# A graph network's attention stage: four message rows multiplied in one VectorE instruction

## The chip, the cores and the metric

The kernel runs on one core of a Trainium2 chip. The metric is the device time of one execution in microseconds. Five engines work side by side, each through its own list in order: TensorE (PE), VectorE (DVE), ScalarE (ACT), GpSimd (POOL) and SyncE (SP). They meet only at semaphores.

## The reference

Four graph layers run one after the other over 6,250 nodes with 256 features and 100,000 edges sorted by destination. Each layer's result is added to its input and normalized. The change touches the first layer only, an attention layer of eight heads:

```python
h = jnp.einsum('nf,fhd->nhd', x, W)
a_src = jnp.sum(h * att_src, axis=-1)
a_dst = jnp.sum(h * att_dst, axis=-1)
e = jax.nn.leaky_relu(a_src[src] + a_dst[dst], NEG_SLOPE)
e_max = jax.ops.segment_max(e, dst, num_segments=N)
e_exp = jnp.exp(e - e_max[dst])
denom = jax.ops.segment_sum(e_exp, dst, num_segments=N)
alpha = e_exp / (denom[dst] + 1e-16)
msg = h[src] * alpha[:, :, None]
out = jax.ops.segment_sum(msg, dst, num_segments=N)
```

Each edge fetches the row of its source node, scales each of the eight heads' 32 features by a weight of that edge, and is summed into its destination.

## The kernel before

The edges are cut into steps of 128, such that all edges of a step end in one tile of 128 nodes. There are 832 steps (`STEPS_PAD`), in 52 groups of 16 (`GROUP`, `S`). The first layer's edge stage, called the heads stage here, does for each step `i`:

- GpSimd gathers the 128 source rows (264 floats each) from a table in memory, one indirect DMA per step (line 1024), into a ring `rows0` of 48 steps. Gather `t` waits for the product of step `t - 48`.
- VectorE multiplies the row's 256 features by the edge's eight weights, each spread over 32 features (line 1339). Both operands are in SBUF.
- TensorE multiplies a one-hot matrix of the destinations by the weighted rows (line 1297). The product goes to one of four banks (`BANKS0`), so it waits for the add of step `i - 4`.
- VectorE adds the product to the sums of the step's node tile (line 1322), three steps later (`LAG0`). The address of the tile is in a register. Each add waits for the product and for the add before it.

The weights of a group's 16 steps come from a chain of small operations (`chain_vector`, `chain_scalar`, `chain_tensor`) that all engines run one group ahead, spread over the 16 steps `k` of the group before: VectorE opens it at `k = 0` (line 1203) once the group's 16 gathers have landed, scans at 3, works on one row at 6 (line 1218, behind ScalarE's line 1119, behind TensorE's transposes at `k = 4`), scans again at 11, and ends it at 13 and 14. The weights of group `g + 1` are made by line 1107 before its first multiply. At the first step of each group the sums are rescaled (lines 1314 and 1316). When a node tile has got its last step, it is closed over the next eight steps, one or two small VectorE operations per step (`close_vector`), and there are 49 such closings.

VectorE's order in a step is: multiply, chain piece, add, closing piece. It is written out by hand, and so is every engine's. Tile numbers reach VectorE by a load of 16 registers (`load_ranks`), once in a group at `k = 11`; one register of them also chooses the column block of `adst` that line 1241 adds.

The other layers use passes of their own (from about 1,236 us on), whose adds share `load_ranks` with the heads stage. A second stage of interest for its rows is the last pass, where line 2015 is a VectorE operation with two SBUF inputs, and line 1863 the gather.

Of the kernel before, what the change touches and what calls it, by code (L numbers as in the profile page):

```python
# [9 lines left out]
ALU = mybir.AluOpType  # L10
# [3 lines left out]
P = 128  # L14
NODES = 6250
EDGES = 100000
FEAT = 256
# [7 lines left out]
GROUP = 16  # L25
# [98 lines left out]
def bcast(ap, axis, shape):  # L124
    return ap.unsqueeze(axis).to_broadcast(shape)
# [134 lines left out]
def build(nc, io):  # L260
    ctx = ExitStack()
    with ctx:
# [569 lines left out]
        def load_ranks(e, name, t0):  # L832
            if name not in rank_regs:
                rank_regs[name] = [e.alloc_register(f"rank{k}") for k in range(2 * GROUP)]
            a = t0 % (2 * GROUP)
            e.load(rank_regs[name][a:a + GROUP], rank_row[0:1, t0:t0 + GROUP])
# [33 lines left out]
        def rank_value(e, name, t):  # L870
            return e.snap(rank_regs[name][t % (2 * GROUP)], min_val=0, max_val=NODE_TILES - 1)
# [8 lines left out]
        BANKS0, LAG0 = 4, 3  # L880
# [100 lines left out]
        def close_scalar(e, i):  # L981
# [15 lines left out]
            "capped first over_in back_states states level_in level_out second_up second node bent_node larger below_node "  # L997
# [7 lines left out]
        weighted0 = s_weighted.take(STEPS_PAD)  # L1005
# [192 lines left out]
        def chain_vector(e, g, k):  # L1198
# [33 lines left out]
            if k == 11:  # L1232
                e.wait_ge(*ch_a.at("begin_col", g))
                e.tensor_tensor_scan(second[:, 0:P], turned3[:, 0:P], turned3[:, 2 * P:3 * P], begin_col[:, 0:1],
# [4 lines left out]
                load_ranks(e, "vector", g * S)  # L1239
                v = rank_value(e, "vector", g * S)  # L1240
                e.tensor_tensor(node_both.rearrange("p (k h) -> p k h", k=2),
                                bank_c[:, 264:264 + 2 * H].rearrange("p (k h) -> p k h", k=2),
                                bcast(adst[:, bass.DynSlice(v * H, H)], 1, [P, 2, H]),
                                ALU.add).then_inc(*ch_v.done("node"))
# [40 lines left out]
        def heads_tensor(e):  # L1285
# [4 lines left out]
            for i in range(STEPS_PAD):  # L1290
# [3 lines left out]
                e.wait_ge(*weighted0(i))  # L1294
# [7 lines left out]
        def heads_vector(e):  # L1302
# [5 lines left out]
            def add(i):  # L1308
                g = i // S
                if i % S == 0 and g:  # L1310
                    e.wait_ge(*ch_v.at("shrink", g))
# [22 lines left out]
            for i in range(STEPS_PAD):  # L1334
                g, k = i // S, i % S
                row = rows0[:, i % (3 * S), :]
                v = row[:, 0:FEAT].rearrange("p (h d) -> p h d", h=H)
                e.wait_ge(*ch_a.at("weights", g))
                e.tensor_tensor(v, v, bcast(row[:, FEAT:ROW0], 2, [P, H, D]), ALU.mult).then_inc(*weighted0.up)  # L1339
# [904 lines left out]
```

## Time and profile before

| | us |
|---|---|
| median of 3 executions | 5310.18 |
| lowest, highest | 5306.78, 5315.72 |
| the profiled execution | 5315.72 |
| its span in the trace | 5313.9 |
| first multiply and last add of the heads stage | 151.5, 1228.6 |
| first gather of the next pass | 1236.1 |

| engine, 900 to 1050 us | busy us of 150 |
|---|---|
| TensorE | 125.92 |
| VectorE | 125.53 |
| ScalarE | 99.94 |
| GpSimd | 114.95 |

An engine's busy time leaves out loads of registers and the issue of instructions. So GpSimd shows 77% busy where gathers follow one another without a pause other than their issue. Instructions of VectorE overlap at their ends: what one adds to the time is the distance from its start to the next one's start, not its duration. "Issue" stands for idle time that nothing in the profile explains.

### The profile page before, as it was taken

What the parts mean: (1) busy time and instruction counts of PE and PEld (TensorE: products, weight loads), DVE (VectorE), ACT (ScalarE), POOL (GpSimd) and SP (SyncE); (2) the same over time, 40 slices, a digit from 0 to 9 for tenths busy, and PEclk for the clock granted to TensorE, in tenths of its full rate; (3) what the DMA queues carried; (4) which work ended last, traced back from release to release, by engine and by line L of the source; (5) the groups of instructions that cost most, each with busy time, mean ns of one, the idle gap of its engine ahead of it and who ended that gap; (6) DMA issues with size and microseconds to landing.
All of it is one profiled execution on the core that took longest, in us unless ns stands there. A gap on an engine that the chain in (4) does not pass through costs nothing.

```text
span 5313.9 us, 86764 instructions
## 1 busy us (share of the span) xinstructions
PE 3931.6 (74%) x13357; PEld 2389.2 (45%) x13357; DVE 3517.2 (66%) x10780; ACT 2554.6 (48%) x6938; POOL 3875.0 (73%) x3995
## 2 busy tenths in 40 slices
PE   6888888887777777677777777777677656666763
PEld 4666666664444444344444443343333333444442
DVE  6789888885554545444444445666666578888887
ACT  1667667664555555455545552000000166666665
POOL 3777777775777777677777776777777677777775
PEclk8889889988899998887777777877888777777776
DMA  5444444443333333443333333333333322222222
GB/s 151 113 122 126 122 126 124 120 121 98 111 112 112 111 112 111 118 139 111 111 112 112 111 112 100 109 109 109 109 108 109 98 57 57 57 57 57 57 57 68
DMA packets 252628, 549.14 MB, mean 103 GB/s; under 512 B 71467, under 2 KB 136235, under 8 KB 252108
## 3 DMA queue, kind: packets, MB, share of 16 engines
q0 software_dynamic: 178752, 478.34, 32.8%
q1 hardware_dynamic: 66972, 58.64, 3.5%
q10 hardware_dynamic: 6384, 6.62, 0.5%
q8 instruction: 157, 2.57, 0.2%
q14 instruction: 363, 2.97, 0.2%
HBM read 501.16 MB, written 42.15 MB: 102 GB/s over the span
## 4 chain that ended last, share of the span: by engine, by line
PE 32%; POOL 22%; DMA 18%; issue 13%; DVE 6%; ACT 6%; SPq 2%; DVEq 1%; ACTq 0%; POOLq 0%
PE bank L1453 18%; POOL scratch L1863 12%; DMA scratch<-tab_x,src_idx 10%; POOL scratch L1399 9%; DMA scratch<-tab_h,src_idx 7%; PE bank L1297 4%; PE bank L172 4%; PE bank L1154 3%; DVE reg_acc L1463 2%; ACT scratch L1066 2%; POOL reg_x L1024 2%; SPq L865 1%; DVE reg_acc L1322 1%; PE bank L1142 1%; PE bank L157 1%
## 5 line engine op out<-in xcount | busy, mean ns | idle before, releaser
L1453 PE MATMUL bank<-scratch 128*128 x4986 | 1946.5, 501 | 739.9 <-SPq L1414 356.6
L1463 DVE TENSOR_TENSOR reg_acc<-reg_acc,bank 128x256 f32 x2493 | 1047.3, 420 | 1368.2 <-PE bank L1453 1310.3
L1399 POOL DMA_INDIRECT scratch<-tab_x,src_idx x1566 | 1494.3, 954 | 533.5 <-issue 259.4
L1453 PEld LDWEIGHTS bank<-scratch 128*128 128x128 f32 x4986 | 961.2, 229 | 1630.2 <-issue 1582.6
L1024 POOL DMA_INDIRECT reg_x<-tab_h,src_idx x832 | 838.7, 1008 | 302.7 <-issue 184.1
L1399 POOL DMA_INDIRECT scratch<-tab_h,src_idx x783 | 746.6, 953 | 264.7 <-issue 153.0
L1863 POOL DMA_INDIRECT scratch<-tab_h,src_idx x783 | 743.0, 949 | 249.3 <-issue 226.8
L1916 PE MATMUL bank<-reg_w,scratch 128*128 128x260 f32 x1664 | 639.8, 527 | 282.7 <-issue 180.1
L1423 ACT ACTIVATE scratch<-iota_row,dst_loc 128x128 f32<-128x128 f32 x1662 | 579.6, 393 | 345.5 <-PE bank L1453 336.1
L1297 PE MATMUL bank<-reg_x,scratch 128*128 128x265 f32 x1664 | 582.4, 461 | 72.7 <-DVE reg_x L1339 70.4
L1916 PEld LDWEIGHTS bank<-reg_w,scratch 128*128 128x128 f32 x1664 | 376.3, 252 | 505.1 <-issue 305.0
L1946 ACT ACTIVATE edge_w<-scratch,attr 128x68 f32 x832 | 288.3, 346 | 311.8 <-SPq L1877 282.0
L1297 PEld LDWEIGHTS bank<-reg_x,scratch 128*128 128x128 f32 x1664 | 305.0, 216 | 205.3 <-DVE reg_x L1339 174.5
L1322 DVE TENSOR_TENSOR reg_acc<-reg_acc,bank 128x265 f32 x832 | 353.5, 425 | 34.2 <-PE bank L1297 23.1
L2032 DVE TENSOR_TENSOR reg_acc<-reg_acc,bank 128x260 f32 x832 | 349.2, 420 | 15.7 <-issue 4.2
L1339 DVE TENSOR_TENSOR reg_x<-reg_x 128x256 f32<-128x256 f32 x832 | 342.6, 412 | 0.4 <-ACT reg_x L1107 0.4
L1439 DVE TENSOR_SCALAR scratch<-iota_row,dst_loc,edge_w 128x128 f32<-128x128 f32 x831 | 322.3, 389 | 6.1 <-issue 6.1
L1931 ACT ACTIVATE scratch<-iota_row,dst_loc 128x128 f32<-128x128 f32 x832 | 319.7, 386 | 3.1 <-DMA tab_h<-reg_w 1.6
L1767 ACT ACTIVATE adst<-adst,small 128x1 f32<-128x1 f32 x49 | 14.4, 294 | 617.4 <-DVE adst L1807 617.4
L2015 DVE SCALAR_TENSOR_TENSOR reg_w<-scratch,attr,edge_w 128x68 f32<-128x68 f32 x832 | 236.3, 284 | 99.9 <-ACT edge_w L1946 87.3
L2063 DVE TENSOR_TENSOR reg_w<-reg_w,bank 128x520 f32<-128x520 f32 x416 | 285.6, 686 | 0.4
L1428 ACT ACTIVATE scratch<-scratch 128x512 f32<-128x512 f32 x416 | 261.7, 629 | 13.1
(313 smaller groups left out, 4364.1 us busy)
## 6 DMA issues: line engine op xcount, KB each, us to landing
scratch<-tab_x,src_idx POOLq DMA_INDIRECT x1566, 2.8
scratch<-tab_h,src_idx POOLq DMA_INDIRECT x1566, 2.7
reg_x<-tab_h,src_idx POOLq DMA_INDIRECT x832
tab_h<-scratch ACTq DMA_DIRECT2D x7, 924.0 KB, 5.2
reg_x<-in_x SPq DMA_DIRECT2D x7, 896.0 KB, 11.3
reg_w<-in_x SPq DMA_DIRECT2D x49, 128.0 KB, 2.3
tab_x<-reg_acc SPq DMA_DIRECT2D x49, 128.0 KB
tab_xs<-reg_w SPq DMA_DIRECT2D x49, 128.0 KB, 2.6
```

Of the source, the lines that this page charges most:

```text
L1024: e.indirect_dma_start(rows0[:, t % (3 * S), 0:ROW0], None, tab_h0, bass.IndirectOffsetOnAxis(ap=src_idx[:, t:t + 1], axis=0)).then_inc(*g ...
L1297: e.matmul(psum[i % BANKS0][:, 0:W0_ROW], hots0[:, i % (2 * S), :], rows0[:, i % (3 * S), :], start=True, stop=True).then_inc(*product0.up)
L1322: e.tensor_tensor(v, v, psum[i % BANKS0][:, 0:W0_ROW], ALU.add).then_inc(*added0.up)
L1339: e.tensor_tensor(v, v, bcast(row[:, FEAT:ROW0], 2, [P, H, D]), ALU.mult).then_inc(*weighted0.up)
L1399: e.indirect_dma_start(ring_rows[:, j % SLOTS, :], None, self.table, bass.IndirectOffsetOnAxis(ap=src_idx[:, j:j + 1], axis=0)).then_inc(* ...
L1423: e.activation(ring_hots[:, i % HOTS, :], iota_row[:, :], ACT.Abs, scale=-1.0, bias=dst_loc[:, i:i + 1]).then_inc(*self.far.up)
L1439: e.tensor_scalar(ring_hots[:, i % HOTS, :], iota_row[:, :], dst_loc[:, i:i + 1], edge_w[:, i:i + 1], ALU.is_equal, ALU.mult).then_inc(*se ...
L1453: e.matmul(self.bank(i), ring_hots[:, i % HOTS, :], rows, start=True, stop=True).then_inc(*self.product.up)
L1463: e.tensor_tensor(v, v, self.bank(i), ALU.add).then_inc(*self.added.up)
L1863: e.indirect_dma_start(ring_rows[:, j % SLOTS, 0:ROW3], None, tab_h3, bass.IndirectOffsetOnAxis(ap=src_idx[:, j:j + 1], axis=0)).then_inc( ...
L1916: e.matmul(psum[i % BANKS][:, 0:WIDE3], hots3[:, i % HOTS, :], scaled3[:, i % 4, :], start=True, stop=True).then_inc(*product3.up)
L2032: e.tensor_tensor(v, v, psum[i % BANKS][:, 0:WIDE3], ALU.add).then_inc(*added3.up)
```

## The change

The weighting of four steps becomes one instruction over four rows of the ring (`AT_ONCE0`), issued at steps 0, 4, 8 and 12 of a group, and TensorE waits for the group of four. The node operation of the chain at `k = 11` moves ahead of the two scans and gets its tile number by a load of one register. The load of 16 registers moves to the add of a group's first step, and holds 16 registers instead of 32.

```diff
--- before.py
+++ after.py
@@ -831,9 +831,9 @@
 
         def load_ranks(e, name, t0):
             if name not in rank_regs:
-                rank_regs[name] = [e.alloc_register(f"rank{k}") for k in range(2 * GROUP)]
-            a = t0 % (2 * GROUP)
-            e.load(rank_regs[name][a:a + GROUP], rank_row[0:1, t0:t0 + GROUP])
+                rank_regs[name] = [e.alloc_register(f"rank{k}") for k in range(GROUP)]
+            n = min(GROUP, STEPS_PAD - t0)
+            e.load(rank_regs[name][0:n], rank_row[0:1, t0:t0 + n])
 
         slot_regs = {}
 
@@ -868,7 +868,7 @@
             return e.snap(end_regs[c % ENDS_AT_ONCE], min_val=1, max_val=STEPS)
 
         def rank_value(e, name, t):
-            return e.snap(rank_regs[name][t % (2 * GROUP)], min_val=0, max_val=NODE_TILES - 1)
+            return e.snap(rank_regs[name][t % GROUP], min_val=0, max_val=NODE_TILES - 1)
 
         def sums_of(e, i, a, b):
             return reg_acc[:, bass.DynSlice(rank_value(e, "vector", i) * ACC_W + a, b - a)]
@@ -877,7 +877,7 @@
 
         S, H, D = GROUP, HEADS0, HEAD0_DIM
         W0_ROW = FEAT + H + 1
-        BANKS0, LAG0 = 4, 3
+        BANKS0, LAG0, AT_ONCE0 = 4, 3, 4
         rows0 = reg_x[:, 0:3 * S * W0_ROW].rearrange("p (s f) -> p s f", f=W0_ROW)
         hots0 = reg_a[:, 0:2 * S * P].rearrange("p (s f) -> p s f", f=P)
         hots_t = reg_a[:, 2 * S * P:2 * S * P + 1024].rearrange("p (s f) -> p s f", s=2)
@@ -994,7 +994,7 @@
 
         got0 = [s_group[k].take(S * len(range(k, GROUPS, 3))) for k in range(3)]
         ch_v = s_chain["vector"].named(
-            "capped first over_in back_states states level_in level_out second_up second node bent_node larger below_node "
+            "capped first over_in back_states states level_in level_out node second_up second bent_node larger below_node "
             "part_added larger_added shrink_less bent shrink below", GROUPS)
         ch_t = s_chain["tensor"].named(
             "turned3 hots0 hots1 dst0 tails hots2 dst1 hots3 begins dst2 dst3 larger", GROUPS)
@@ -1002,7 +1002,7 @@
             "upright hot0 kept3 hot1 kept_hot0 step_masks hot2 kept_tails kept_hot1 hot3 begins kept_hot2 kept_hot3 "
             "begin_col part shrink weights", GROUPS)
         far0 = s_far.take(STEPS_PAD)
-        weighted0 = s_weighted.take(STEPS_PAD)
+        weighted0 = s_weighted.take(STEPS_PAD // AT_ONCE0)
         product0, added0 = s_edge.take(STEPS_PAD), s_added.take(STEPS_PAD)
         scaled0, denscaled0 = s_scaled.take(GROUPS - 1), s_denscaled.take(GROUPS - 1)
 
@@ -1230,18 +1230,20 @@
                                 ALU.max).then_inc(*ch_v.done("level_in"))
                 e.tensor_copy(level[:, (g + 1) % 2, 0:H], st[:, 0, S - 1, :]).then_inc(*ch_v.done("level_out"))
             if k == 11:
+                if "head" not in rank_regs:
+                    rank_regs["head"] = e.alloc_register("head_rank")
+                e.load(rank_regs["head"], rank_row[0:1, g * S:g * S + 1])
+                v = e.snap(rank_regs["head"], min_val=0, max_val=NODE_TILES - 1)
                 e.wait_ge(*ch_a.at("begin_col", g))
+                e.tensor_tensor(node_both.rearrange("p (k h) -> p k h", k=2),
+                                bank_c[:, 264:264 + 2 * H].rearrange("p (k h) -> p k h", k=2),
+                                bcast(adst[:, bass.DynSlice(v * H, H)], 1, [P, 2, H]),
+                                ALU.add).then_inc(*ch_v.done("node"))
                 e.tensor_tensor_scan(second[:, 0:P], turned3[:, 0:P], turned3[:, 2 * P:3 * P], begin_col[:, 0:1],
                                      ALU.add, ALU.max).then_inc(*ch_v.done("second_up"))
                 e.tensor_tensor_scan(second[:, P:2 * P][:, back], turned3[:, P:2 * P][:, back],
                                      turned3[:, 2 * P:3 * P][:, back], begin_col[:, 1:2], ALU.add,
                                      ALU.max).then_inc(*ch_v.done("second"))
-                load_ranks(e, "vector", g * S)
-                v = rank_value(e, "vector", g * S)
-                e.tensor_tensor(node_both.rearrange("p (k h) -> p k h", k=2),
-                                bank_c[:, 264:264 + 2 * H].rearrange("p (k h) -> p k h", k=2),
-                                bcast(adst[:, bass.DynSlice(v * H, H)], 1, [P, 2, H]),
-                                ALU.add).then_inc(*ch_v.done("node"))
                 e.wait_ge(*ch_v.at("node", g))
                 leaky(e, node_both).then_inc(*ch_v.done("bent_node"))
                 e.wait_ge(*ch_v.at("second", g))
@@ -1291,7 +1293,7 @@
                 g, k = i // S, i % S
                 if g + 1 < GROUPS:
                     chain_tensor(e, g + 1, k, True)
-                e.wait_ge(*weighted0(i))
+                e.wait_ge(*weighted0(i // AT_ONCE0))
                 if i >= BANKS0:
                     e.wait_ge(*added0(i - BANKS0))
                 e.matmul(psum[i % BANKS0][:, 0:W0_ROW], hots0[:, i % (2 * S), :], rows0[:, i % (3 * S), :], start=True,
@@ -1307,7 +1309,10 @@
 
             def add(i):
                 g = i // S
+                if i % S == 0 and g == 0:
+                    load_ranks(e, "vector", 0)
                 if i % S == 0 and g:
+                    load_ranks(e, "vector", i)
                     e.wait_ge(*ch_v.at("shrink", g))
                     e.wait_ge(*added0(i - 1))
                     v = sums_of(e, i, 0, FEAT).rearrange("p (h d) -> p h d", h=H)
@@ -1333,10 +1338,12 @@
                 chain_vector(e, 0, k)
             for i in range(STEPS_PAD):
                 g, k = i // S, i % S
-                row = rows0[:, i % (3 * S), :]
-                v = row[:, 0:FEAT].rearrange("p (h d) -> p h d", h=H)
-                e.wait_ge(*ch_a.at("weights", g))
-                e.tensor_tensor(v, v, bcast(row[:, FEAT:ROW0], 2, [P, H, D]), ALU.mult).then_inc(*weighted0.up)
+                if k % AT_ONCE0 == 0:
+                    rows = rows0[:, i % (3 * S):i % (3 * S) + AT_ONCE0, :]
+                    v = rows[:, :, 0:FEAT].rearrange("p s (h d) -> p s h d", h=H)
+                    e.wait_ge(*ch_a.at("weights", g))
+                    e.tensor_tensor(v, v, bcast(rows[:, :, FEAT:ROW0], 3, [P, AT_ONCE0, H, D]),
+                                    ALU.mult).then_inc(*weighted0.up)
                 if g + 1 < GROUPS:
                     chain_vector(e, g + 1, k)
                 if i >= LAG0:
```

VectorE's order, as the program has it, from step 14 of a group (line 1269 in the old numbering, 1271 in the new) into step 1 of the next. Line 1322 is the add (1327 in the changed kernel), 1339 the multiply (1345), 1203 the chain's opening; `ISA` computes an address from a register. Before:

```order
L1322 TENSOR_TENSOR reg_acc<-reg_acc,bank 128x265
L1339 TENSOR_TENSOR reg_x<-reg_x 128x256
L1269 TENSOR_TENSOR scratch<-scratch 128x128
L871 ISA
L1322 TENSOR_TENSOR reg_acc<-reg_acc,bank 128x265
L1339 TENSOR_TENSOR reg_x<-reg_x 128x256
L871 ISA
L1322 TENSOR_TENSOR reg_acc<-reg_acc,bank 128x265
L1339 TENSOR_TENSOR reg_x<-reg_x 128x256
L1203 TENSOR_TENSOR scratch<-reg_x,scratch 128x128
L871 ISA
L1322 TENSOR_TENSOR reg_acc<-reg_acc,bank 128x265
```

And changed:

```order
L1327 TENSOR_TENSOR reg_acc<-reg_acc,bank 128x265
L1271 TENSOR_TENSOR scratch<-scratch 128x128
L871 ISA
L1327 TENSOR_TENSOR reg_acc<-reg_acc,bank 128x265
L871 ISA
L1327 TENSOR_TENSOR reg_acc<-reg_acc,bank 128x265
L1345 TENSOR_TENSOR reg_x<-reg_x 128x4x256
L1203 TENSOR_TENSOR scratch<-reg_x,scratch 128x128
L871 ISA
L1327 TENSOR_TENSOR reg_acc<-reg_acc,bank 128x265
```

One multiply of 4x256 stands where four stood, one per step, and the adds of steps 1 to 3 behind it have no multiply between them.

VectorE at `k = 11`, from the second pair of scans (lines 1234 and 1236; 1242 and 1244 in the changed kernel) to the operation before the next add; `TENSOR_LOAD` is the load of tile numbers, and 1241 (1238) the node operation. Before:

```order
L1234 SCALAR_TENSOR_TENSOR scratch<-scratch 128x128
L1236 SCALAR_TENSOR_TENSOR scratch<-scratch 128x128
L836 TENSOR_LOAD step_rows
L871 ISA
L1241 TENSOR_TENSOR scratch<-bank,adst 128x16
L1196 SCALAR_TENSOR_TENSOR scratch<-scratch 128x16
L1248 TENSOR_TENSOR scratch<-scratch 128x128
L1251 TENSOR_TENSOR scratch<-scratch 128x8
```

And changed:

```order
L1235 TENSOR_LOAD step_rows
L1238 ISA
L1238 TENSOR_TENSOR scratch<-bank,adst 128x16
L1242 SCALAR_TENSOR_TENSOR scratch<-scratch 128x128
L1244 SCALAR_TENSOR_TENSOR scratch<-scratch 128x128
L1196 SCALAR_TENSOR_TENSOR scratch<-scratch 128x16
L1250 TENSOR_TENSOR scratch<-scratch 128x128
L1253 TENSOR_TENSOR scratch<-scratch 128x8
```

The load and the node operation now stand ahead of the scans, and the load takes one register.

VectorE at `k = 3`, from the first pair of scans to the first add of a group, with the rescaling (lines 1314 and 1316; 1319 and 1321) between. Before:

```order
L1207 SCALAR_TENSOR_TENSOR scratch<-scratch 128x128
L1208 SCALAR_TENSOR_TENSOR scratch<-scratch 128x128
L871 ISA
L1314 TENSOR_TENSOR reg_acc<-reg_acc,scratch 128x256
L871 ISA
L1316 TENSOR_TENSOR reg_acc<-reg_acc,scratch 128x8
L871 ISA
L1322 TENSOR_TENSOR reg_acc<-reg_acc,bank 128x265
L942 RECIPROCAL small<-small 128x8
```

And changed:

```order
L1207 SCALAR_TENSOR_TENSOR scratch<-scratch 128x128
L1208 SCALAR_TENSOR_TENSOR scratch<-scratch 128x128
L836 TENSOR_LOAD step_rows
L871 ISA
L1319 TENSOR_TENSOR reg_acc<-reg_acc,scratch 128x256
L871 ISA
L1321 TENSOR_TENSOR reg_acc<-reg_acc,scratch 128x8
L871 ISA
L1327 TENSOR_TENSOR reg_acc<-reg_acc,bank 128x265
```

The load of 16 registers now stands between the scans and the rescaling.

## Rows read from the trace of the kernel before

**Rows 1.** Gathers of the heads stage, groups of instructions from 150 to 1230 us.

```profile
L1024 POOL DMA_INDIRECT reg_x<-tab_h,src_idx x802 | 795.7, 992 | 244.4 <-issue 175.2 <-PE bank L1297 69.2
```

**Rows 2.** GpSimd's waits in the whole program: total us, times, longest us.

```profile
POOL reg_x L1024 <- issue: 184.1, 604, 0.3
POOL reg_x L1024 <- PE bank L1297: 69.2, 227, 0.3
```

**Rows 3.** VectorE's waits from 150 to 1230 us: total us, times, longest us.

```profile
DVE scratch L1218 <- ACT scratch L1119: 50.1, 37, 2.9
DVE scratch L1203 <- DMA reg_x<-tab_h,src_idx: 38.8, 21, 3.3
DVE reg_acc L1322 <- PE bank L1297: 23.1, 35, 1.8
DVE scratch L1241 <- issue: 6.2, 14, 1.0
```

**Rows 4.** Instructions of line 1203, 150 to 1230 us: ns min/median/max, first to last start.

```profile
L1203 DVE TENSOR_TENSOR scratch<-reg_x,scratch x51: 277/283/293, 153.9 to 1195.5; 128x128 f32<-128x128 f32 x51
```

**Rows 5.** Timeline of GpSimd (two gathers) and VectorE (line 1203): start, duration.

```profile
1003.07 1.07 POOL L1024 DMA_INDIRECT reg_x<-tab_h,src_idx  x1 [0.30 <-issue]
...
1006.00 0.29 DVE L1203 TENSOR_TENSOR scratch<-reg_x,scratch 128x128 f32<-128x128 f32 x1 [2.01 <-DMA reg_x<-tab_h,src_idx]
...
1188.38 1.20 POOL L1024 DMA_INDIRECT reg_x<-tab_h,src_idx  x1 [0.30 <-issue]
```

**Rows 6.** Timeline of VectorE in mid-stage, one multiply between the two.

```profile
1010.40 0.42 DVE L1322 TENSOR_TENSOR reg_acc<-reg_acc,bank 128x265 f32 x1
...
1011.08 0.42 DVE L1322 TENSOR_TENSOR reg_acc<-reg_acc,bank 128x265 f32 x1
```

**Rows 7.** Timeline of VectorE at the end of the program.

```profile
5272.42 2.01 DVE L2108 TENSOR_TENSOR reg_acc<-reg_acc,edge_w 128x1792 f32<-128x1792 f32 x1
5274.36 2.04 DVE L230 BATCH_NORM_STATS2 scratch<-reg_x 128x6 f32<-128x256 f32 x6
```

**Rows 8.** Timeline of VectorE, the last two adds of the heads stage.

```profile
1227.94 0.43 DVE L1322 TENSOR_TENSOR reg_acc<-reg_acc,bank 128x265 f32 x1 [0.22 <-DVE reg_acc L1322]
1228.59 0.43 DVE L1322 TENSOR_TENSOR reg_acc<-reg_acc,bank 128x265 f32 x1 [0.22 <-DVE reg_acc L1322]
```

**Rows 9.** Timeline of VectorE, one operation of a tile closing among the steps.

```profile
1196.78 0.42 DVE L946 TENSOR_TENSOR reg_acc<-reg_acc,small 128x256 f32<-128x256 f32 x1
1197.11 0.42 DVE L1339 TENSOR_TENSOR reg_x<-reg_x 128x256 f32<-128x256 f32 x1
```

**Rows 10.** Timeline of VectorE: a 16-register load (first pair), a one-register load (second).

```profile
4448.28 0.28 DVE L2015 SCALAR_TENSOR_TENSOR reg_w<-scratch,attr,edge_w 128x68 f32<-128x68 f32 x1
4449.17 0.43 DVE L2027 TENSOR_TENSOR reg_acc<-reg_acc,adst 128x260 f32 x1 [0.60 <-issue]
...
93.06 0.21 DVE L812 COPY edge_w<-bank 128x64 f32<-128x64 f32 x1
93.41 0.36 DVE L801 COPY adst<-scratch 128x392 f32 x1
```

**Rows 11.** Timeline of VectorE: the first of two scans, and what follows both.

```profile
1008.44 0.41 DVE L1207 TENSOR_TENSOR_SCAN scratch<-scratch 128x128 f32<-128x128 f32 x1
...
1009.09 0.40 DVE L1314 TENSOR_TENSOR reg_acc<-reg_acc,scratch 128x256 f32 x1
```

**Rows 12.** Instructions of the last pass, 4400 to 5200 us.

```profile
L1863 POOL DMA_INDIRECT scratch<-tab_h,src_idx x639 | 606.5, 949 | 194.8 <-issue 184.1 <-SPq L1875 10.7
L2015 DVE SCALAR_TENSOR_TENSOR reg_w<-scratch,attr,edge_w 128x68 f32<-128x68 f32 x680 | 193.1, 284 | 66.3 <-ACT edge_w L1946 54.6 <-issue 9.6
```

**Rows 13.** Timeline of GpSimd and VectorE as the heads stage begins.

```profile
112.47 14.12 POOL L1024 DMA_INDIRECT reg_x<-tab_h,src_idx  x1 [0.30 <-issue]
114.20 11.15 DVE L1325 MEMSET reg_acc<- 128x13312 f32 x1 [2.70 <-issue]
```

**Rows 14.** TensorE's wait for the multiplies, 150 to 1230 us.

```profile
PE bank L1297 <- DVE reg_x L1339: 70.4, 147, 2.2
```

## The prediction

> **What bounds the kernel now.** Only the heads stage is changed, some 1,080 of 5,314 us; what follows starts when its sums are complete. What the stage's own engines do decides it, so I ask first who sets the pace there. In the groups of instructions GpSimd's gathers come first: 802 of them take 795.7 us and the idle time before them 244.4 us, together 1,040.1 us, or 1.297 us a gather and 20.75 us for a group of 16 [rows 1]. Then I look at what GpSimd waited for. No gap is longer than 0.3 us, whether it is put down to issue (184.1 us over 604 times, 0.305 each) or to a product (69.2 over 227, 0.305 each): the named product lands inside a gap that is there anyway [rows 2]. The ring of 48 steps never holds a gather up. GpSimd runs without a stop and nothing in this change shortens its list.
>
> VectorE follows. From the first to the last opening of a chain are 50 groups in 1195.5 - 153.9 = 1,041.6 us, 20.83 us a group [rows 4], the same pace. In the list of its waits 38.8 us (21 times) are for gathers, 0.76 us a group over 51 [rows 3]. Without them it would need 20.83 - 0.76 = 20.07 us. Its other waits are for the chain: 50.1 us for line 1119's tails, 23.1 us for products [rows 3]. So the bound is GpSimd by a small margin: VectorE may grow by 20.75 - 20.07 = 0.68 us a group before the stage gets longer, and if it shrinks, it waits more for gathers.
>
> **Part 1, the batch.** Two adds with one multiply between are 11.08 - 10.40 = 0.68 us apart, so each instruction of 256 elements costs 0.34 us on VectorE, though it lasts 0.42 [rows 6]. A product over 1,792 elements with the same kind of spread operand lasts 2.01 us, and its follower starts 1.94 us after it [rows 7]. Between the two sizes that is (1.94 - 0.34) / 1,536 = 1.042 ns an element, so 1,024 elements cost 0.34 + 768 x 0.001042 = 1.14 us. Four multiplies cost 1.36 us. The batch saves 0.22 us, 0.88 us a group, 46 us over 208 batches if VectorE were the bound. The bounds of this price are an exact 0.34 for the fixed part (saving 46) and the full duration of each (4 x 0.42 [rows 9] against 0.42 + 0.80 = 1.22: 0.46 a batch, 96 us); I take the first, since the starts show the overlap.
>
> The Trainium skill, "VectorE: DVE Perf Modes", section on the TRN2 errata, says that many small tiles pay the SBUF latency each and a large one once, and gives (N + 151) / 0.96 ns for such an fp32 operation. For the durations the trace agrees: 2.02 us for 1,792 elements against the row's 2.01. By it the batch would save 3 x 157 = 472 ns. The distance of the starts says that half of that is already hidden.
>
> **Part 2, adds that stand behind one another.** This is what the diff does not say. Each add waits for the add before it. Today a multiply stands between, which hides the wait. Where nothing did, the adds were 1228.59 - 1227.94 = 0.65 us apart, 0.22 of it idle and put down to the add itself [rows 8], against 0.34. Each bare pair costs 0.31 us. A batch leaves three pairs bare, 12 a group: the adds of steps 1-3, 5-7, 9-11, 13-15. Chain work longer than 0.31 stands before those of 3, 6, 11 and 13, and before that of 14 stands a small operation of about 0.20. Seven are bare: 7 x 0.31 + 0.11 = 2.28 us. Closings fill some: each runs over eight steps, four of them with an operation of 0.33 us [rows 9], four with about 0.1, so a closing hides up to 4 x 0.31 + 4 x 0.1 = 1.64 us, and 7 of 16 steps need it: 0.72 x 49 / 52 = 0.68 us. Left: 1.60 us a group.
>
> **Part 3, the loads.** With 16 registers loaded between, two starts are 0.89 us apart, of which 0.60 idle; with one register 0.35, of which 0.14 idle [rows 10]. The 16-register load now stands behind the scans of k = 3, which occupy 9.09 - 8.44 = 0.65 us [rows 11]: 0.24 us stay bare (bounds 0 and 0.60). The one-register load costs 0.15. The old load's idle time goes, 6.2 / 51 = 0.12 [rows 3]. Sum: +0.27 us a group. The node operation itself only moves; ScalarE's and TensorE's part of the chain that waits for the maximum of the scans gets it about 0.1 us later, with work of theirs in between.
>
> **Sum.** -0.88 + 1.60 + 0.27 = +0.99 us of VectorE work a group. Not all of it lengthens the group. What stands between the scans of k = 3 and the wait at k = 6 (load 0.24, pair of step 5 0.31, batch -0.22, so 0.33) goes into a wait of 50.1 / 51 = 0.98 us that TensorE and ScalarE set. Of the pairs of steps 7, 9 and 10 some goes into the product waits (0.45 us a group); I take 0.25. Left: about +0.4 us, 20.5 us a group against GpSimd's 20.75. VectorE, slower than before, is still the faster of the two.
>
> TensorE gets four rows at once, later by up to 1.14 - 0.34 = 0.8 us for the first of them, earlier for the last. It waited 70.4 us for multiplies [rows 14], while VectorE worked; VectorE's first add of a new row comes after three adds, 1.0 to 1.9 us behind the batch, time for one product. I put nothing down for it.
>
> **The end of the stage.** The last gather ends at 1189.58, the chain opens at 1195.5, 5.9 us later, where 1.86 us is the least when VectorE was waiting (1004.14 to 1006.00) [rows 4, 5]. So the tail starts up to 4 us late, and would start up to 4 us earlier if VectorE is on time, which I cannot decide. Then come 32 steps without gathers. Group 50 costs +0.4; group 51 has no chain, so its 12 pairs are covered by closings alone: 12 x 0.31 - 1.5 - 0.88 = +1.3. Together +1.7 against -4 to 0: I take 0. The sum is 5315.7 + 0 for an execution like the profiled one, with 1.8 us around the span as now. That execution was the slowest of three, 5.5 us over the median; carried to the median the forecast is 5310 us. Its own range is -6 to +10: 5304 to 5320.
>
> **Rivals.**
>
> *VectorE passes GpSimd (slower).* The mechanism is part 2. It decides from +0.68 us a group. If no wait takes anything in and the load stays bare for 0.60, the growth is 0.99 + 0.36 = 1.35, 0.67 over: x 51 = +34 us, 5344. If closings also cover nothing, it is +69, 5379. For it: the work of 0.99 alone is over the margin, and half of my absorption is judgement. Against it: 73 us of chain waits stand in the list that extra work can fill.
>
> *The long multiply holds the gathers up (slower).* The gathers of this stage take 992 ns, those of the last pass 949 [rows 1, 12]: 43 ns x 802 = 34 us. If that comes from multiplies that hold a path GpSimd needs, the wait goes with the square of the hold: 832 x 0.34² = 96 against 208 x 1.14² = 270, 2.8 times, +62 us, 5372. For it: one gather took 14.12 us across a memset of 11.15 us [rows 13]. Against it: the last pass has its own operation with two SBUF inputs every step and gathers of 949 [rows 12].
> The Trainium skill, "SBUF — State Buffer", "Who interferes with whom", says that a VectorE operation with two SBUF inputs blocks GpSimd's reads of SBUF for its whole length, but infers that descriptor writing isn't hit. By the first half this rival is right, by the second wrong; the 949 ns row sides with the second.
>
> *The gathers get shorter (faster).* If the 34 us come with the number of VectorE's SBUF instructions instead, three quarters of the multiplies' part goes: up to -26 us, 5284. Nothing in the rows ties it to them.
>
> *VectorE was the bound after all (faster).* Then 46 us go and part 2 does not bite: 5264. Against it: rows 2, where the gathers have no gap to give back.
>
> **How the numbers follow.** Forecast 0.73; VectorE passes 0.10; held gathers 0.05; shorter gathers 0.08; VectorE bound 0.04. About 0.2% (10.6 us) can be told from no change. Faster takes the last two, 0.12, slower the first two, 0.15, same 0.73. The range must leave out no more than 2 in 10: 5296 leaves out most of the faster cases, 5332 takes in a VectorE that passes by 0.4 us a group (+20).
>
> **What the profile would show.** Right: batches of about 1.22 us with the next start 1.14 after them; bare adds 0.65 apart; gathers still at 1.29 to 1.30 us with no gap over 0.3; VectorE's busy time lower by about 95 us (832 x 0.42 - 208 x 1.22), with tens of us of idle time before adds that is put down to the add before; first multiply to last add 1,077 us within 6. Wrong: gaps of GpSimd over 0.3 put down to products, with VectorE's wait for gathers gone (it has passed), or gathers with another mean than 992 ns. Anything that moves by over 10 us outside the heads stage would be none of my steps.

## The result and the profile after: 65 us slower

| | before | after |
|---|---|---|
| median of the runs, us | 5312.69 (4 runs, 5306.78 to 5315.72) | 5377.81 (4 runs, 5374.31 to 5383.28) |
| ratio | 1 | 1.0131 (95% interval 1.0119 to 1.0143) |
| profiled execution, its own time / its span, us | 5315.72 / 5313.9 | 5385.96 / 5384.2 |
| start of the last gather of the heads stage, us | 1188.4 | 1264.1 |
| start of its last add, us | 1228.59 | 1303.17 |

The forecast was 5310 with a range to 5332. The time lies near two of the prediction's rival figures: 5372 for the held gathers, which had a chance of 0.05, and 5379 for a VectorE that passes GpSimd and whose closings cover nothing. The time alone does not tell them apart; the profile does.

The granted clock did not change (0.82 before, 0.818 after). The page of the changed kernel has these lines on the span, the engines (busy us, share, instructions) and the gathers (busy us, mean ns, idle us before them):

```profile
span 5384.2 us, 86244 instructions
PE 3920.0 (73%) x13357; PEld 2399.7 (45%) x13357; DVE 3510.3 (65%) x10156; ACT 2556.1 (47%) x6938; POOL 3946.7 (73%) x3995
L1024 POOL DMA_INDIRECT reg_x<-tab_h,src_idx x832 | 914.9, 1100 | 302.6 <-issue 177.6
```

VectorE is busy for 3510.3 us instead of 3517.2, and GpSimd for 3946.7 instead of 3875.0. An engine whose instructions the change doesn't touch has 72 us more to do. In the groups of the heads stage, 150 to 1300 us, the three kinds of instruction on which the argument stands are:

```profile
L1024 POOL DMA_INDIRECT reg_x<-tab_h,src_idx x801 | 871.0, 1087 | 244.0 <-issue 168.5 <-PE bank L1299 75.6
...
L1327 DVE TENSOR_TENSOR reg_acc<-reg_acc,bank 128x265 f32 x827 | 354.5, 429 | 72.9 <-DVE reg_acc L1327 33.1 <-PE bank L1299 23.6 <-DVE reg_acc L1321 7.8
...
L1345 DVE TENSOR_TENSOR reg_x<-reg_x 128x1024 f32<-128x1024 f32 x208 | 252.7, 1215 | 0.4 <-ACT reg_x L1107 0.4
```

The first line answers to [rows 1]. The idle time before a gather is what it was, 244.0 / 801 = 0.305 us. The mean duration went from 992 to 1087 ns. One gather with its gap now takes 1115.0 / 801 = 1.392 us, and 16 of them 22.27 us where they took 20.75. Over 802 gathers the difference of 0.095 us makes 76 us, and the last gather starts 75.7 us later. GpSimd's waits, which answer to [rows 2]:

```profile
POOL reg_x L1024 <- issue: 177.6, 583, 0.3
POOL reg_x L1024 <- PE bank L1299: 75.6, 248, 0.3
```

The longest is still 0.3 us. GpSimd stands still nowhere in the stage, so no product is late and VectorE has not passed it. It works without a stop on instructions that take longer. The openings of the chains keep its pace, as in [rows 4]:

```profile
L1203 DVE TENSOR_TENSOR scratch<-reg_x,scratch x51: 280/292/316, 153.1 to 1268.0; 128x128 f32<-128x128 f32 x51
```

These are 50 groups in 1114.9 us, 22.30 us each. VectorE's waits in the stage, beside [rows 3]:

```profile
DVE scratch L1203 <- DMA reg_x<-tab_h,src_idx: 90.8, 41, 4.6
...
DVE reg_acc L1327 <- DVE reg_acc L1327: 33.1, 151, 0.6
DVE scratch L1218 <- ACT scratch L1119: 29.1, 34, 2.8
DVE reg_acc L1327 <- PE bank L1299: 23.6, 54, 1.4
DVE reg_acc L1319 <- DVE scratch L1208: 22.2, 45, 0.9
```

The wait for gathers went from 38.8 to 90.8 us, 1.78 us a group. VectorE alone would need 22.30 - 1.78 = 20.52 us a group. I had worked out 20.5.

Last, two stretches of the timeline of the changed kernel, GpSimd's and VectorE's (start, duration, idle time before):

```profile
520.10 0.94 POOL L1024 DMA_INDIRECT reg_x<-tab_h,src_idx  x1 [0.30 <-issue]
521.35 1.82 POOL L1024 DMA_INDIRECT reg_x<-tab_h,src_idx  x1 [0.30 <-PE bank L1299]
523.48 0.95 POOL L1024 DMA_INDIRECT reg_x<-tab_h,src_idx  x1 [0.30 <-issue]
...
521.14 1.22 DVE L1345 TENSOR_TENSOR reg_x<-reg_x 128x1024 f32<-128x1024 f32 x1
522.27 0.43 DVE L1327 TENSOR_TENSOR reg_acc<-reg_acc,bank 128x265 f32 x1
522.92 0.43 DVE L1327 TENSOR_TENSOR reg_acc<-reg_acc,bank 128x265 f32 x1 [0.22 <-DVE reg_acc L1327]
523.57 0.43 DVE L1327 TENSOR_TENSOR reg_acc<-reg_acc,bank 128x265 f32 x1 [0.22 <-DVE reg_acc L1327]
```

The multiply runs from 521.14 to 522.36. The gather before it ends at 521.04 after 0.94 us. The one that starts inside it, at 521.35, takes 1.82 us and ends at 523.17, 0.81 us after the multiply. The next takes 0.95 us again. In the kernel before, the same thing can be seen once one looks for it (VectorE, then GpSimd):

```profile
511.95 0.42 DVE L1339 TENSOR_TENSOR reg_x<-reg_x 128x256 f32<-128x256 f32 x1
...
512.16 1.02 POOL L1024 DMA_INDIRECT reg_x<-tab_h,src_idx  x1 [0.30 <-PE bank L1297]
```

The multiply ends at 512.37, the gather at 513.18, again 0.81 us later. It took 1.02 us, only 0.07 more than others, since a small multiply holds for a short time. Read over the whole stage, the gathers that start under a multiply take together 25 us more than 0.945 us each in the kernel before, and 101 us more in the changed one. That difference is the 76 us. It also corrects the sentence ahead of the prediction that the engines meet only at semaphores: no semaphore stands between this multiply and this gather.

### The profile page after: what moved, and what is told of

It is laid out like the page before. It is cut to its first block, busy times and chain, and to the rows that moved or that the text cites. A ratio compares the mean times of both kernels' runs of the same rounds, so it can differ in the third digit from the quotient of the medians.

```text
span 5384.2 us, 86244 instructions
## 1 busy us (share of the span) xinstructions
PE 3920.0 (73%) x13357; PEld 2399.7 (45%) x13357; DVE 3510.3 (65%) x10156; ACT 2556.1 (47%) x6938; POOL 3946.7 (73%) x3995
## 4 chain that ended last, share of the span: by engine, by line
PE 32%; POOL 22%; DMA 20%; issue 13%; DVE 5%; ACT 5%; SPq 2%; DVEq 1%; ACTq 0%; POOLq 0%
PE bank L1460 18%; DMA scratch<-tab_x,src_idx 12%; POOL scratch L1870 11%; POOL scratch L1406 8%; DMA scratch<-tab_h,src_idx 7%; PE bank L1299 4%; POOL reg_x L1024 4%; PE bank L172 4%; PE bank L1154 2%; DMA reg_x<-tab_h,src_idx 2%; DVE reg_acc L1470 2%; ACT scratch L1066 1%; PE bank L1142 1%; SPq L865 1%; PE bank L157 1%
## 5 line engine op out<-in xcount | busy, mean ns | idle before, releaser
L1024 POOL DMA_INDIRECT reg_x<-tab_h,src_idx x832 | 914.9, 1100 | 302.6 <-issue 177.6
L1430 ACT ACTIVATE scratch<-iota_row,dst_loc 128x128 f32<-128x128 f32 x1662 | 580.7, 393 | 346.2 <-PE bank L1460 336.5
L1299 PEld LDWEIGHTS bank<-reg_x,scratch 128*128 128x128 f32 x1664 | 317.9, 222 | 222.2 <-DVE reg_x L1345 119.9
L1938 ACT ACTIVATE scratch<-iota_row,dst_loc 128x128 f32<-128x128 f32 x832 | 319.8, 386 | 2.9 <-DMA tab_h<-reg_w 1.6
L1066 ACT ACTIVATE scratch<-iota_row,dst_loc 128x128 f32<-128x128 f32 x832 | 264.8, 389 | 0.0
```

The lines of the kernel that those rows point to most:

```text
L1024: e.indirect_dma_start(rows0[:, t % (3 * S), 0:ROW0], None, tab_h0, bass.IndirectOffsetOnAxis(ap=src_idx[:, t:t + 1], axis=0)).then_inc(*g ...
L1299: e.matmul(psum[i % BANKS0][:, 0:W0_ROW], hots0[:, i % (2 * S), :], rows0[:, i % (3 * S), :], start=True, stop=True).then_inc(*product0.up)
L1430: e.activation(ring_hots[:, i % HOTS, :], iota_row[:, :], ACT.Abs, scale=-1.0, bias=dst_loc[:, i:i + 1]).then_inc(*self.far.up)
L1938: e.activation(hots3[:, i % HOTS, :], iota_row[:, :], ACT.Abs, scale=-1.0, bias=dst_loc[:, i:i + 1]).then_inc(*far3.up)
```

## The experiments

Three theories stood against each other. *The hold*: a gather that starts while VectorE runs a multiply with both inputs in SBUF waits for that multiply to end. *The pattern*: four sets of rows taken and given back at once disturb the rhythm of the ring. *The added work*: VectorE's bare adds set the pace.

### The batch without the rest of the change

The kernel before, with the batch alone; node operation and loads stay where they were.

```diff
-                e.wait_ge(*weighted0(i))
+                e.wait_ge(*weighted0(i // AT_ONCE0))
...
-                e.tensor_tensor(v, v, bcast(row[:, FEAT:ROW0], 2, [P, H, D]), ALU.mult)
+                if k % AT_ONCE0 == 0:
+                    rows = rows0[:, i % (3 * S):i % (3 * S) + AT_ONCE0, :]
+                    e.tensor_tensor(v, v, bcast(rows[:, :, FEAT:ROW0], 3, [P, AT_ONCE0, H, D]), ALU.mult)
```

> The kernel before with the batch of four alone; node operation and load stay where they were. P, N and D all: the whole loss is the batch's, 5370 to 5382, gathers 1.09.

Measured: 5377.05 us where the kernel before took 5307.72, ratio 1.0132 (1.0115 to 1.0149), as expected. The gathers in its groups of instructions:

```profile
L1024 POOL DMA_INDIRECT reg_x<-tab_h,src_idx x802 | 861.8, 1075 | 244.3 <-issue 176.7 <-PE bank L1297 67.6
```

The mean of 1075 ns is a little under the 1.09 us expected. The whole loss belongs to the batch. Moving the loads and the node operation costs nothing that these intervals can show; the next run puts it at 9 us or less.

### One, two and eight rows in an instruction

The changed kernel with one number changed, here to 1, in the others to 2 and to 8.

```diff
-        BANKS0, LAG0, AT_ONCE0 = 4, 3, 4
+        BANKS0, LAG0, AT_ONCE0 = 4, 3, 1
```

> One row per multiply again; the moved node operation and both loads stay. Theory P (a gather that begins while a multiply with two SBUF inputs streams waits for its end): hold 0.27 us as before, so gathers at 0.99 us mean and the time of before, 5312 within 8. Theory N (the lengthening comes from the pattern of four: product releases and matmuls in bursts): also 5312. Theory D (VectorE's own added work sets the pace): the loads cost 0.27 us a group, still under the margin of 0.68: 5312. If the moved load were the cause, this kernel would be near 5378.

> Two rows per multiply. P: the wait of all gathers is n x hold^2 / (2 x 1.3 us): 832 x 0.267^2 gives 23 us, 416 x 0.533^2 gives 45, 208 x 1.067^2 gives 91; scaled so that 23 to 91 is the 76 us measured, two rows cost +25 over before: 5338, gather mean about 1,023 ns. N: something between 5312 and 5378, with no number of its own. D: eight bare pairs of adds a group for twelve: two thirds of +65, 5355, and gaps of GpSimd over 0.3 us.

> Eight rows per multiply. P: the hold is 2.13 us, longer than a gather's period of 1.3, so nearly every one of 104 multiplies makes one gather wait 2.13 - 0.65 = 1.48 us: 154 us, 131 over before's 23, so 5440 to 5460, gathers at 1.15 to 1.18 us mean and single ones up to 3.1 us. D: 14 bare pairs for 12, VectorE saves 0.4 us more: within 15 us of 5378. N: a burst of eight, somewhat over 5378.

In this series the kernel before took 5316.57 us. Measured: one row 5319.31 us, 1.0007 (0.9997 to 1.0016). Two rows 5336.66, 1.0046 (1.0030 to 1.0061). Eight rows 5445.96, 1.0241 (1.0224 to 1.0258). All three came out where the hold put them; for two and eight rows the added work would have given other times (5355, and within 15 us of 5378). The gathers of the stage with one row:

```profile
L1024 POOL DMA_INDIRECT reg_x<-tab_h,src_idx x801 | 794.8, 992 | 244.1 <-issue 170.4 <-PE bank L1299 73.8
```

With two rows:

```profile
L1024 POOL DMA_INDIRECT reg_x<-tab_h,src_idx x802 | 815.2, 1016 | 244.3 <-issue 172.1 <-PE bank L1299 72.2
```

With eight rows:

```profile
L1024 POOL DMA_INDIRECT reg_x<-tab_h,src_idx x802 | 921.4, 1149 | 244.5 <-issue 167.3 <-PE bank L1299 77.1
```

The idle time is 0.30 us a gather in all three, no gap is longer than 0.3 us, and only the duration grows. How long a gather is held was read from those that start while a multiply runs. In every kernel their duration falls by 1.0 us for each us that they start later, so that all end at the same distance from the multiply's end. The exception are some that start within the first 0.03 us of a multiply: in the changed kernel seven such gathers took 0.94 to 0.95 us. The longest hold is what this line gives at the multiply's start above 0.945 us, which gathers clear of a multiply take:

| elements in one multiply | longest hold, us | n x hold² / (2 x 1.3), us | mean gather, ns | (mean - 963) x 802, us |
|---|---|---|---|---|
| 256 (before; one row) | 0.30 | 23 | 992 | 23 |
| 512 (two rows) | 0.55 | 45 | 1016 | 43 |
| 1,024 (four rows) | 1.09 | 91 | 1087 | 99 |
| 2,048 (eight rows) | 2.15 | see text | about 1149 | 149 |

The hold is elements x 1.04 ns to within 0.03 us, the same slope as that of the multiply's own duration in part 1. The third column is the expected sum of all holds: n multiplies (832, 416, 208), a gather every 1.3 us at any point of them, and a wait that is half of the hold in the mean, with 1.04 ns an element for the hold. The last column needs a mean without any hold. 963 is the one with which the first row comes out at 23 us; the next experiments measure 958. For 2,048 elements the hold is longer than the distance of two gathers, each multiply holds one of them for 2.13 - 0.65 us in the mean, and 104 x 1.48 = 154 us.

One stretch of the kernel with eight rows, VectorE and GpSimd:

```profile
756.42 2.25 DVE L1345 TENSOR_TENSOR reg_x<-reg_x 128x2048 f32<-128x2048 f32 x1
...
756.53 2.97 POOL L1024 DMA_INDIRECT reg_x<-tab_h,src_idx  x1 [0.30 <-issue]
```

A single gather of 2.97 us, and it ends at 759.50, 0.83 us after the multiply. This follows from the hold alone. A disturbed ring would show in the gaps, and more work of VectorE in waits of GpSimd for products; neither is there.

### Four rows, but half of the elements

The pattern and the waits of the change stay, and the multiply is as short as that of two rows. It leaves the weighting of the other 128 features out.

```diff
-                    v = rows[:, :, 0:FEAT].rearrange("p s (h d) -> p s h d", h=H)
+                    v = rows[:, :, 0:FEAT // 2].rearrange("p s (h d) -> p s h d", h=H // 2)
-                    e.tensor_tensor(v, v, bcast(rows[:, :, FEAT:ROW0], 3, [P, AT_ONCE0, H, D]),
+                    e.tensor_tensor(v, v, bcast(rows[:, :, FEAT:FEAT + H // 2], 3, [P, AT_ONCE0, H // 2, D]),
```

> Four rows per multiply, but only the first 128 of each row's 256 features are weighted (the other half is left out). The pattern of four stays, and the hold is halved to 0.53 us. P: 208 x 0.533^2 / 2.6 = 23 us of waits, what 832 single rows cost: 5312 within 8, gather mean 0.99. N: the pattern is unchanged, so 5378 and 1.09. D: VectorE saves 2.1 us a group, so 5312 as well; D is told apart by the gathers of after, not here.

Measured: 5322.56 us, 1.0002 (0.9991 to 1.0012). Gathers of the stage, then GpSimd's wait for products:

```profile
L1024 POOL DMA_INDIRECT reg_x<-tab_h,src_idx x802 | 789.5, 984 | 246.3 <-issue 177.1 <-PE bank L1299 69.2
```

```profile
POOL reg_x L1024 <- PE bank L1299: 69.2, 221, 1.6
```

The hold rule gives 208 x 0.53² / 2.6 = 22 us here, as much as before the change, and mean and time come back. The pattern of four by itself costs nothing. The longest wait for a product is now 1.6 us, the first over 0.3 in this series, a sign of what was to come with fewer banks. The time is 2.6 us above what was expected (5312 within 8), in a series whose kernel before took 5316.57 us.

### The second input in PSUM

To keep the long multiply and take away one SBUF input, the weights are written a second time, into a PSUM bank. All eight banks are in use, so a product bank had to go; a control has three banks and the weights where they were (the first pair of lines alone).

```diff
-        BANKS0, LAG0, AT_ONCE0 = 4, 3, 4
+        BANKS0, LAG0, AT_ONCE0 = 3, 3, 4
+                    e.activation(psum[3][:, 0:P], both[:, 0:P], ACT.Exp)
-                    e.tensor_tensor(v, v, bcast(rows[:, :, FEAT:ROW0], 3, [P, AT_ONCE0, H, D]),
+                    some = psum[3][:, 0:P].rearrange("p (s h) -> p s h", h=H)[:, k:k + AT_ONCE0, :]
+                    e.tensor_tensor(v, v, bcast(some, 3, [P, AT_ONCE0, H, D]),
```

> Four rows per multiply, but the weights are read from a PSUM bank of their own, so the multiply has one SBUF input; the product ring shrinks from four banks to three, and ScalarE writes the weights twice. P: the gathers no longer wait for the multiply: mean about 0.96 us (what is left comes from scans and closings), while the multiply still lasts 1.2 us. GpSimd's pace falls to about 20.2 us a group, below VectorE's 20.5, so VectorE's added adds set the pace for the first time: 5290 to 5312. N: gathers stay at 1.09 and the time near 5378 or over.

> Control for the run before it: the changed kernel with three product banks and the weights in SBUF. P: gathers 1.09 as in the changed kernel, time 5375 to 5390, as GpSimd stays the bound and three banks only eat VectorE's slack. N: the same.

> Two rows per multiply with the weights in PSUM, three banks. P: gathers 0.96, GpSimd 20.2 us a group; VectorE pays eight bare pairs for twelve, so it comes out between e5 and 15 us below it: 5280 to 5305, the fastest of all. N: as the two-row kernel, 5337.

The kernel before took 5307.72 us in this series. Measured: weights in PSUM 5434.01 us, 1.0246 (1.0210 to 1.0282); the control 5440.22, 1.0264 (1.0237 to 1.0292); two rows with the weights in PSUM 5445.15, 1.0256 (1.0212 to 1.0301). All three times missed what was expected. The durations did not. Weights in PSUM, groups of the stage, then a stretch of VectorE and GpSimd, then GpSimd's wait for products:

```profile
L1024 POOL DMA_INDIRECT reg_x<-tab_h,src_idx x802 | 768.7, 958 | 385.4 <-PE bank L1300 230.5 <-issue 154.9
...
L1347 DVE TENSOR_TENSOR reg_x<-reg_x,bank 128x1024 f32<-128x1024 f32 x207 | 250.0, 1208 | 0.6 <-ACT reg_x L1108 0.6
```

```profile
785.67 1.21 DVE L1347 TENSOR_TENSOR reg_x<-reg_x,bank 128x1024 f32<-128x1024 f32 x1
...
785.89 0.94 POOL L1024 DMA_INDIRECT reg_x<-tab_h,src_idx  x1 [0.40 <-PE bank L1300]
```

```profile
POOL reg_x L1024 <- PE bank L1300: 230.5, 296, 2.8
```

The multiply has the same shape and lasts 1,208 ns against 1,215. A gather starts 0.22 us into it and takes 0.94 us; of 148 gathers that start under such a multiply none took over 0.95. The mean is 958 ns, below that of the kernel before. With two rows it is 962. The control, with both inputs in SBUF:

```profile
L1024 POOL DMA_INDIRECT reg_x<-tab_h,src_idx x802 | 868.1, 1082 | 271.8 <-issue 174.0 <-PE bank L1299 97.9
```

It stays at 1082. So for this multiply the second input in SBUF decides, and not its length or the number of banks. That instructions with fewer SBUF inputs never hold a gather is not shown. The kernel before has one that did, ahead of the stage's first multiply (VectorE, then GpSimd):

```profile
100.30 1.03 DVE L588 TENSOR_SCALAR reg_acc<-scratch 128x1664 f32<-128x1664 f32 x1
...
100.47 1.68 POOL L1024 DMA_INDIRECT reg_x<-tab_h,src_idx  x1 [0.30 <-issue]
```

This instruction has one tensor as input, in SBUF, and spends 0.62 ns an element. The gather ends at 102.15, again 0.82 us after it. No run here tests why.

What the kernel with PSUM saves in durations it loses in waits: 230.5 us for products, up to 2.8 us each. Its control, whose gathers are 124 ns longer, takes the same time, and VectorE's waits for gathers fell from 90.8 us in the changed kernel to 2.1 (7.3 in the control). So with three banks GpSimd is no longer the bound, and the time says nothing on the hold. That the loop from VectorE over the chain and TensorE back to VectorE's adds is the bound instead, and which part of it, is my reading; no run takes it apart.

### A bank taken from the chain

The other way to free one: the chain turns its four tables through one bank instead of two, and the fourth turn moves behind `begins`. Four product banks stay. In the first two kernels the weights go to the freed bank, `psum[5]`, by the same added and changed lines as in the last experiment. The second is the kernel before with one row per multiply (row 15 of a group is weighted beside row 14). The control has the single turning bank alone, on the kernel before.

```diff
-        bank_t, bank_3, bank_d, bank_c = (psum[4], psum[5]), ...
+        bank_t, bank_3, bank_d, bank_c = (psum[4], psum[4]), ...
-            "turned3 hots0 hots1 dst0 tails hots2 dst1 hots3 begins dst2 dst3 larger", GROUPS)
+            "turned3 hots0 hots1 dst0 tails hots2 dst1 begins hots3 dst2 dst3 larger", GROUPS)
```

> The changed kernel with the weights read from a PSUM bank, and all four product banks kept; the bank is won by turning the one-hot matrices through one bank instead of two, so the chain of the next group has a wait more on TensorE. P: gathers 0.96 us, GpSimd free to run at 20.2 us a group, and the time is set by the loop of VectorE, TensorE and ScalarE: my sum of 20.5 us a group says 5300 to 5325, over 50 us under the changed kernel. If the one turning bank costs over 0.5 us a group, gaps of GpSimd put down to products show it, and the time may reach 5340. N: 5378 and gathers of 1.09.

> One row per multiply with the weights in PSUM (row 15 of a group is weighted beside row 14), one turning bank, the rest as before. P: gathers 0.96 us, and VectorE has one bare pair of adds a group instead of twelve, so it is 0.4 us a group or 20 us faster than e9: 5290 to 5310. If it is no faster than e9, the bare adds cost nothing here.

> Control: the kernel before with one turning bank, weights in SBUF, one row per multiply. The chain's later transposes eat slack that GpSimd's pace gives: 5312 to 5325, gathers 0.99. The difference to e10 is what PSUM weights bring to single rows.

These three ran on another chip, where the kernel before took 6566.31 us, the granted clock was 0.73 instead of 0.82, and waits came up that no other profile of this case has; they can be compared with each other only. Measured: four rows with weights in PSUM 6636.56 us, 1.0108 (1.0089 to 1.0127). One row with weights in PSUM 6615.43, 1.0070 (1.0046 to 1.0095). The control 6638.66, 1.0106 (1.0088 to 1.0125). The mean gather is 960, 953 and 975 ns in this order. The control alone costs as much as the four rows do, so the missing turning bank and not the batch seems to make their loss there; one row with free gathers is perhaps a little better than its control, though the two intervals overlap. Against the kernel before, all three came out above what was expected of them. The first of them was run once more on a chip like the others:

> The kernel of e9 once more, on a chip where the kernel before takes about 5310 us (in the group of e9 it took 6566, with waits at every semaphore that the other traces do not have). P: gathers 0.96 us, so GpSimd's own pace is 20.2 us a group, and what is left is the loop with one turning bank: 5310 to 5345, below the changed kernel's 5378. N: 5378 or over.

Measured: 5430.73 us, 1.0225 (1.0208 to 1.0242), expected 5310 to 5345: missed. Groups of the stage, GpSimd's wait for products, and VectorE's two longest waits of the stage:

```profile
L1024 POOL DMA_INDIRECT reg_x<-tab_h,src_idx x802 | 768.4, 958 | 386.2 <-PE bank L1299 226.4 <-issue 159.8
```

```profile
POOL reg_x L1024 <- PE bank L1299: 226.4, 281, 4.0
```

```profile
DVE scratch L1218 <- ACT scratch L1120: 67.0, 48, 3.4
DVE scratch L1238 <- ACT scratch L1095: 53.0, 36, 3.1
```

The gathers take 958 ns, and 226 us of waiting for products eat that and more. The chain is late at lines 1218 and 1238, whose waits were 29.1 and 5.9 us in the changed kernel. I put that down to the missing bank for the turns; its control was not run on such a chip. What a batch of four brings while gathers run free and the chain keeps all its banks stays open; none of the kernels tried has both, and none beats the kernel before.

## Why the prediction was wrong

**The bound** was named rightly: GpSimd's gathers, without gaps, before and after. The step that failed is the sentence behind it, "nothing in this change shortens its list". It was taken to mean that nothing makes the list longer either: GpSimd's 20.75 us a group went into the forecast unchanged, and what the longer multiply does to the gathers was put at nothing. The number of gathers stayed, their duration went from 992 to 1087 ns, and the group from 20.75 to 22.27 us.

**The rival with the held gathers** was what happened, and it was put at 0.05. Its law was right, the square of the hold: 91 - 23 = 68 us by elements, 62 us in the prediction, 76 in the profile. That the prediction's figure comes so near is in part luck. It took 0.34 us for the hold of a small multiply, which gives a factor of 2.8 where elements give 4, and it laid all of 34 us on the multiplies, where 23 us by the rule and 25 by the trace belong to them; the two errors pull against each other.

The chance was wrong, on one row. The operation with two SBUF inputs in the last pass with its gathers of 949 ns [rows 12] was read as evidence that such operations hold nothing. That operation has 68 elements, and its hold by the rule found here is 0.07 us, which is too short to be seen in any mean. Gather by gather it is there: of 129 that start under line 2015, 20 take more than 0.96 us, up to 1.03. The row could not tell the theories apart. The gather of 14.12 us beside a memset of 11.15 [rows 13] was put aside. It does not bear out the rule of two inputs, since a memset reads nothing and its record begins 1.73 us after the gather's, and what held that gather stays open; but it did show that work of VectorE can go with a gather far longer than 949 ns. Hidden in the kernel before was also a direct test: gathers under a multiply that end 0.81 us after it.

The Trainium skill, "SBUF — State Buffer", "Who interferes with whom", has the rule that a VectorE operation with two SBUF inputs keeps GpSimd from reading SBUF for its whole length. The runs agree: 1.09 us for 1,024 elements, and nothing with the second input in PSUM. The same section infers that the writing of descriptors isn't hit by such an operation. The prediction took that to speak for all that GpSimd does in a gather, and it does not: a gather also takes its row numbers from SBUF (`src_idx`), and its duration grew from 992 to 1087 ns. Which of the two was held, the reading of row numbers or the writing, no run here tells.

**Part 1.** Right. The next start after a batch comes 522.27 - 521.14 = 1.13 us later (1.14 worked out), and the mean duration is 1,215 ns (1.22).

**Part 2.** The distance is right: 522.92 - 522.27 = 0.65 us, 0.22 of it idle. The count is not confirmed. The waits show 151 bare adds after an add, 3 a group, where 1.60 / 0.31 = 5 were counted; some others stand under waits for products (54).

**Part 3 and the sum.** Right as a sum, 20.52 us a group by the trace against 20.5. It had no effect, since GpSimd's pace had meanwhile gone to 22.27. "VectorE passes GpSimd" was therefore wrong too, though its upper figure of 5379 is nearer to the time than any other of the prediction: no gap of GpSimd is over 0.3 us. As the chain waits changed with the pace (line 1218 from 50.1 to 29.1 us, a new one of 22.2 at line 1319), the agreement holds for the sum and not for each term.

**VectorE's busy time** was to fall by 95 us and fell by 6.9. The multiplies' sum did fall, from 832 x 0.42 to 252.7 us. But consecutive instructions overlap, and the busy time counts an overlap once. The 95 us were worked out from full durations, which contradicts the prediction's own price by starts.

**The end of the stage.** Right: 39.1 us from the last gather's start to the last add's, 40.2 before. Outside the stage 4.3 us are gone, under the 10 that were named as a limit. First multiply to last add took 1,152 us and not 1,077: the 75 us of the gathers.

## What to carry to other kernels

Ask of every change to an engine off the bound not only how much time it takes there, but what it locks while it runs. Here each multiply of n elements with two SBUF inputs held a gather up by as much as n x 1.04 ns, and as long as the hold is shorter than the distance of two gathers, its sum goes with the square of the length: four times longer and four times fewer costs four times as much. Small multiplies are the better form while GpSimd's gathers set the pace. And before a row is taken as evidence against a mechanism, work out how large the effect would be in just that row: if it is below what the row can show, the row says nothing.

## What the runs showed of the hardware

- A gather that starts during a VectorE multiply with both inputs in SBUF ends 0.81 to 0.83 us after the multiply, at 256, 1,024 and 2,048 elements, or takes the 0.945 us that it takes alone if that ends later. The longest hold was 0.30, 0.55, 1.09 and 2.15 us for 256, 512, 1,024 and 2,048 elements. The hold bites at a gather's start only. Of the changed kernel's gathers 145 had begun when a multiply of 1,024 elements started: 107 took at most 1.0 us, and the other 38 (up to 1.16) had all started under another VectorE instruction with both inputs in SBUF, such as the scans.
- With the second input in PSUM the same multiply lasted as long (1,208 against 1,215 ns) and held no gather (0.94 us).
- The kernel before already paid for this: 992 ns for its gathers against 958 with the weights in PSUM, 27 us over 802 gathers. It could not be had here: on the chips where the kernel before takes 5,308 to 5,309 us, the kernels with a bank freed took 5,431 us and more.
